# Who multiplies Q and K with the rope's cosines in layer 1: VectorE or GpSimd

## The chip, the cores and the metric

The kernel runs on one core of a Trainium2 chip. The metric is the device time of one execution in microseconds; less is better. The core's engines run side by side, each with an instruction stream of its own, and wait for one another on semaphores: TensorE (PE in the profile) for matrix products, VectorE (DVE), ScalarE (ACT), GpSimd (POOL), and SyncE (SP), which issues DMAs.

## The reference, cut to what matters

Two transformer layers over 1024 tokens of width 256. Each layer is attention (16 heads of 16) and then a mixture of 32 experts with 4 per token, each behind a layer norm, with a residual added. Only layer 1's attention turns Q and K by the rope:

```python
def _apply_rope(x, sin, cos):
    xp = x.reshape(x.shape[:-1] + (x.shape[-1] // 2, 2))
    swapped = jnp.stack((-xp[..., 1], xp[..., 0]), axis=-1).reshape(x.shape)
    return x * cos + swapped * sin
...
q = jnp.einsum('bsd,hkd->bhsk', x, wq.reshape(H, dk, D))   # k, v likewise
sin, cos = _rope_tables(S, dk, THETA, x.dtype)
q = _apply_rope(q, sin, cos)
k = _apply_rope(k, sin, cos)
scores = jnp.einsum('bhqk,bhsk->bhqs', q, k) / jnp.sqrt(jnp.asarray(dk, x.dtype))
```

So for each of Q and K there are a swap of neighbours, a product with sines, a product with cosines, and a sum. After it come causal scores, softmax, the product with V, and the output projection.

## The kernel before, in words

The loop `for L in range(2)` in each engine's stream runs the two layers. Q and K are kept transposed: 256 rows (head dimensions) by 1024 tokens, in two blocks of 128 rows, `m` = 0 and 1. `qkf(m, j)` is block `m` of Q (`j` = 0) or of K (`j` = 1), 128x1024 in f32. Block 0 lies in memory that the profile calls w_sgu, block 1 in xn. Head groups 0 and 1 live in block 0, groups 2 and 3 in block 1.

In layer 1 the work around the change goes so, and each engine does its share strictly in this order:

- TensorE makes block 0's Q and K in four products of 512 tokens (L830), then V for 8 token tiles (L846), then block 1's Q and K in four more (L830), and after that the maxima of the scores (L875, L878) for head group 0.
- ScalarE copies the four products of block 0 out of PSUM (L1234). Each copy adds 1 to the semaphore `qk_sb1`. It then goes through a fixed list: the first bf16 part of Q (`split`, L1246), V's tiles 0 to 3 (`v_out`, L1253), the second part of Q, V's tiles 4 to 7, the first part of K, and one copy of block 1, the second part of K, and the other copies of block 1.
- VectorE turns block 0 (L1519 to L1528): first Q, then K. For each it waits for two copies, shuffles neighbours into `swapped` (L1516), multiplies with the sines (L1526), multiplies with the cosines into `by_cos` (L1527), and adds (L1528), which adds 1 to `roped`. Between K's shuffle and K's sines it takes the first part off Q (`take_part`, L302). After K's sum it takes the remaining parts off Q and K (three more at L302), then shuffles Q of block 1, and then reads score maxima out of PSUM (L1556).
- GpSimd waits for the last of these `take_part`s (`left`), and then turns block 1 by itself: cosines (L710), sines (L712), sum (L714), for Q and for K. Between layer 0's last expert and that wait it has nothing to do.
- SyncE sends the bf16 parts of block 0 to QA and KA by DMA (L539), each as soon as ScalarE or VectorE has made it, in the order Q first part, Q second, K first, Q third, K second, K third. Head group 0's maxima wait for all of these.

`ch.step` gives an instruction a semaphore increment; `ch.link` does the same and makes the engine wait for it before its next instruction. The VectorE stretch, with the helper that takes a part off:

```python
def take_part(eng, L, m, j, part):                                   # L296
    eng.wait_ge(S(f"parts_p{part}_{L}"), 2 * m + j + 1)
    q = qkf(m, j)
    eng.tensor_tensor(q if part == 1 else by_rows(part_of(m, j, 2)), q, by_rows(part_of(m, j, part - 1)),
                      ALU.subtract)\
       .then_inc(left(L, m, j, part)[0], 1)                          # L302
...
dve.wait_ge(S("rope"), 32)                                           # L1519
for j in range(2):
    q, by_sin = qkf(0, j), by_rows(swapped[:, j, :])
    dve.wait_ge(S("qk_sb1"), (j + 1) * NC)                           # NC = 2
    ch.link(turn_pairs(j, 0))                                        # the shuffle
    if j == 1:
        take_part(dve, 1, 0, 0, 1)
    ch.step(v.tensor_tensor(by_sin, by_sin, by_rows(sin_t[:, :]), ALU.mult))
    ch.link(v.tensor_tensor(by_rows(by_cos[:, j, :]), q, by_rows(cos_t[:, :]), ALU.mult))
    v.tensor_tensor(q, by_rows(by_cos[:, j, :]), by_sin, ALU.add).then_inc(S("roped"), 1)
take_part(dve, L, 0, 0, 2)
take_part(dve, L, 0, 1, 1)
take_part(dve, L, 0, 1, 2)
```

Other lines that the rows name: L732 is GpSimd's causal mask over a block of probabilities. L769 to L784 (GpSimd) and L1792, L1873 (VectorE) make layer 0's token lists. L1625 and L1630 (VectorE) belong to layer 1's RMS norm. L1294 is ScalarE's exponential.

Of the kernel before, what the change touches and what calls it, by code (L numbers as in the profile page):

```python
# [10 lines left out]
ALU = mybir.AluOpType  # L11
# [13 lines left out]
NC = T // CH  # L25
# [252 lines left out]
def build(nc, a, out):  # L278
    ctx = ExitStack()
    with ctx:  # L280
        sems = {}

        def S(name):
            if name not in sems:
                sems[name] = ctx.enter_context(nc.semaphore(name))
            return sems[name]

        def left(L, m, j, part):

            who, those = ("pool", POOL_PARTS) if (m, j) in POOL_PARTS else ("dve", DVE_PARTS)  # L290
            return S(f"left{part}_{who}"), len(those) * L + those.index((m, j)) + 1
# [6 lines left out]
# [8 lines that stand above are left out]
        def sb(name, shape, dt=F32):  # L306
            return ctx.enter_context(nc.sbuf_tensor(name, shape, dt))
# [29 lines left out]
        cos_t = sb("cos_t", [P, T])  # L337
        sin_t = sb("sin_t", [P, T])
# [14 lines left out]
        def by_rows(t):  # L353

            return t.rearrange("p (c n) -> p c n", n=D)
# [6 lines left out]
        def qkf(m, j):  # L362

            return xn[:, TPC * j:TPC * (j + 1), 0:D] if m else qk_first[:, j, :, :]
# [9 lines left out]
        by_cos = X[:, 2 * T:4 * T].rearrange("p (a t) -> p a t", a=2)  # L374
# [278 lines left out]
        def _(pool):  # L653
            ch = Chain(pool, S("pool_own"))
# [43 lines left out]
            for L in range(2):  # L698
# [3 lines left out]
                if L == 0:  # L702
                    ch.link(pool.memset(V[:, :, :, DH + 1:], 0.0))
                    pool.memset(V[:, :, :, DH:DH + 1], 1.0).then_inc(S("v_pad"), 1)
                else:

                    pool.wait_ge(*left(1, 0, 1, 2))
                    for j in range(2):
                        pool.wait_ge(S("qk_sb1"), (2 + j + 1) * NC)
                        ch.step(pool.tensor_tensor(by_rows(cos_late), qkf(1, j), by_rows(cos_t[:, :]), ALU.mult))  # L710
                        pool.wait_ge(S("swapped"), j + 1)
                        ch.link(pool.tensor_tensor(by_rows(swapped_late[:, j, :]), by_rows(swapped_late[:, j, :]),  # L712
                                                   by_rows(sin_t[:, :]), ALU.mult))
                        pool.tensor_tensor(qkf(1, j), by_rows(cos_late), by_rows(swapped_late[:, j, :]), ALU.add)\  # L714
                            .then_inc(S("roped"), 1)
                        pool.wait_ge(S("roped"), 2 + j + 1)
                for j in range(2):
                    take_part(pool, L, 1, j, 1)
                for st, (_, _, c, b) in enumerate(STEPS):
                    if L == 0 and st == PHASE_AT[4]:  # L720

                        pool.wait_ge(S("qa_rows0_3"), 16 * 2 * NPROD)
                        pool.memset(bias_parts, 0.0).then_inc(S("bias_parts"), 1)
                    if not DIAGONAL[st]:
                        continue
                    if st in (2, 3):

                        take_part(pool, L, 1, st - 2, 2)
                    off = b * P - c * CH
                    block_p = probs[:, st % PB, :, off:off + P]  # L730
                    pool.wait_ge(S(f"exp{L}"), 2 * st + 2)
                    pool.affine_select(out=block_p, in_=block_p, compare_op=ALU.is_ge, fill=0.0, base=0,  # L732
                                       pattern=[[0, HG], [1, P]], channel_multiplier=-1).then_inc(S(f"masked{L}"), 1)
# [66 lines left out]
        def _(pe):  # L800
# [17 lines left out]
            for L in range(2):  # L818
# [44 lines left out]
                def unit(x):  # L863
# [3 lines left out]
                    if n >= RB:  # L867
                        pe.wait_ge(*out_of(UNITS[n - RB]))
                    if x[0] == "max":
                        _, g, u = x  # L870
                        _, i, h0, nh, s0, w = MAX_UNITS[u]
                        for j in range(nh):
                            h = HG * g + h0 + j
# [3 lines left out]
                            if diag:  # L877
                                mm = pe.matmul(ps[:, bank, (j + 1) * w - P:(j + 1) * w], identb[:, :], mask_q[:, :],  # L878
                                               start=False, stop=True)
                    elif x[0] == "rows":  # L880
                        _, g, c = x
                        pe.wait_ge(S(f"neg_max{L}"), PHASES.index((g, c)) + 1)
                        for i in range(TPC):
# [552 lines left out]
        def _(dve):  # L1436
            ch = Chain(dve, S("dve_own"))
            v = nc.vector
# [60 lines left out]
            for L in range(2):  # L1499
# [13 lines left out]
                def turn_pairs(j, m):  # L1513

                    swap = [x ^ HG for x in range(32)]
                    return v.stream_shuffle(by_rows((swapped_late if m else swapped)[:, j, :]), qkf(m, j), swap)  # L1516

                if L == 1:
# [3 lines that stand above are left out]
                        dve.wait_ge(S("qk_sb1"), (j + 1) * NC)  # L1522
                        ch.link(turn_pairs(j, 0))
                        if j == 1:
                            take_part(dve, 1, 0, 0, 1)
                        ch.step(v.tensor_tensor(by_sin, by_sin, by_rows(sin_t[:, :]), ALU.mult))  # L1526
                        ch.link(v.tensor_tensor(by_rows(by_cos[:, j, :]), q, by_rows(cos_t[:, :]), ALU.mult))  # L1527
                        v.tensor_tensor(q, by_rows(by_cos[:, j, :]), by_sin, ALU.add).then_inc(S("roped"), 1)  # L1528
                if L == 0:
                    take_part(dve, 0, 0, 0, 1)  # L1530
# [541 lines left out]
```

## Time and profile before

| | us |
|---|---|
| median of 3 runs | 777.88 |
| lowest and highest of them | 777.22, 784.95 |
| the profiled execution's own time | 778.84 |
| its span, first to last instruction | 777.1 |

The profiled execution is one more run, 0.96 us above the median; 1.7 us of it lie outside the span. All rows below are of this execution, and their times count from its span's start. A row of a timeline gives the start, the time until the end, the engine and line, and in square brackets how long the engine had been idle before it and what ended that. Rows with xN merge N instructions that follow each other; starts and ends are then of the whole.

### The profile page before, as it was taken

The page shows a single profiled execution, that of the slowest core. Times are in us where ns is not written, and L with a number is a line of the kernel's source. Part 1 is how long each engine was busy: PE and PEld are TensorE (multiplying, and loading weights), DVE is VectorE, ACT ScalarE, POOL GpSimd, SP SyncE. Part 2 cuts the span into 40 slices and gives each one's busy share as a digit, 9 for nine tenths or more (in the row PEclk, how much of TensorE's full clock was granted, in tenths as well). Part 3 has the DMA queues.
Part 4 walks back from the last instruction along what each step waited for, and adds up shares of the span by engine and source line. Part 5 has one row for each costly group of instructions (what it writes and reads, how often), then busy time and mean ns, then how long its engine had stood idle before and what let it go on. Part 6 is the DMA issues. An engine that isn't in the chain of part 4 may idle for free.

```text
span 777.1 us, 13393 instructions
## 1 busy us (share of the span) xinstructions
PE 676.1 (87%) x4375; PEld 438.1 (56%) x4375; DVE 487.7 (63%) x1357; ACT 323.1 (42%) x684; POOL 250.5 (32%) x293
## 2 busy tenths in 40 slices
PE   3988999999578999999963978999998899999981
PEld 2533443345347999999842533343343456999970
DVE  4489899454683444444466889899526885343447
ACT  3553465764124333222331533564676231333322
POOL 3140111211047776444410183010211002677620
PEclk9999999999679999999996979999999999999995
DMA  3443210150009999999770244003000530499662
GB/s 98 139 132 110 77 35 0 44 175 28 27 29 301 322 322 312 299 299 306 228 228 0 88 134 159 15 4 113 2 1 1 183 113 15 138 293 305 217 222 70
DMA packets 60263, 108.54 MB, mean 140 GB/s; under 512 B 11173, under 2 KB 37115, under 8 KB 60068
## 3 DMA queue, kind: packets, MB, share of 16 engines
q1 hardware_dynamic: 52500, 93.86, 37.6%
q0 software_dynamic: 7632, 13.80, 5.5%
q8 instruction: 37, 0.61, 0.3%
q14 instruction: 30, 0.25, 0.1%
q10 hardware_dynamic: 64, 0.03, 0.0%
HBM read 79.98 MB, written 19.79 MB: 128 GB/s over the span
## 4 chain that ended last, share of the span: by engine, by line
PE 56%; DVE 25%; DMA 6%; ACT 4%; issue 4%; POOL 2%; SPq 1%; ACTq 0%; POOLq 0%; DVEq 0%
PE ps L1125 13%; DVE mx L1556 11%; PE ps L957 7%; PE ps L943 6%; PE ps L875 5%; PE ps L1138 4%; PE ps L989 4%; PE ps L1140 4%; DMA outs<-X,token 3%; PE ps L1069 3%; ACT X L1294 2%; PE ps L908 1%; PE ps L1101 1%; SPq L539 1%; PE ps L830 1%
## 5 line engine op out<-in xcount | busy, mean ns | idle before, releaser
L1556 DVE TENSOR_REDUCE mx<-ps 128x1 f32<-128x512 f32 (+3 forms) x304 | 180.5, 656 | 25.9 <-PE ps L878 17.5
L1294 ACT ACTIVATE X<-ps 128x1024 f32<-128x1024 f32 (+1 forms) x192 | 146.6, 809 | 87.9 <-PE ps L943 87.5
L875 PE MATMUL ps<-KA,QA 112*128 112x512 bf16 (+3 forms) x384 | 113.1, 345 | 8.6 <-DVE mx L1556 3.9
L760 POOL DMA_INDIRECT outs<-X,token x95 | 95.0, 1000 | 73.6 <-DVE X L1929 59.4
L732 POOL TENSOR_SCALAR_AFFINE_SELECT X<-X 128x512 f32<-128x512 f32 x64 | 40.9, 639 | 219.0 <-ACT X L1294 219.0
L943 PE MATMUL ps<-QA,KA 114*128 114x512 bf16 (+3 forms) x384 | 93.8, 330 | 5.9 <-ACT X L1294 4.0
L1125 PE MATMUL ps<-QA,KA 128*128 x756 | 95.0, 275 | 1.9 <-ACT QA L1400 1.5
L1125 PEld LDWEIGHTS ps<-QA,KA 128*128 128x128 f32 x756 | 91.9, 192 | 4.6 <-issue 2.8
L1916 DVE TENSOR_TENSOR X<-ps,X 128x128 f32<-128x128 f32 x95 | 27.7, 292 | 101.4 <-ACT X L1411 101.0
L752 POOL DMA_INDIRECT V<-token_rows,row_of_slot x64 | 66.8, 1043 | 66.8 <-DVE row_of_slot L1829 42.9
L875 PEld LDWEIGHTS ps<-KA,QA 112*128 112x128 bf16 x384 | 36.9, 100 | 84.9 <-DVE mx L1556 60.6
L957 PE MATMUL ps<-X,V 128*32 128x512 f32 (+3 forms) x768 | 81.1, 497 | 0.4 <-ACT X L1301 0.4
L1409 ACT ACTIVATE X<-ps 128x128 f32<-128x128 f32 x95 | 26.4, 278 | 117.2 <-PE ps L1125 117.2
L943 PEld LDWEIGHTS ps<-QA,KA 114*128 114x128 bf16 x384 | 30.2, 99 | 49.8 <-ACT X L1294 30.8
L1138 PE MATMUL ps<-KA,X 128*128 128x256 f32 x190 | 57.1, 382 | 0.7 <-DVE X L1920 0.2
L1140 PE MATMUL ps<-X 128*128 128x256 f32 x190 | 56.5, 379 | 0.0
L989 PE MATMUL ps<-xT,w_sgu 128*128 128x512 f32 x112 | 54.2, 628 | 2.2 <-DVE QA L1700 2.2
L1929 DVE COPY X<-ps 128x256 f32<-128x256 f32 x95 | 40.4, 425 | 20.5 <-DMA outs<-X,token 16.3
L878 PE MATMUL ps<-mask_q,identb 128*128 128x128 bf16 x256 | 51.9, 230 | 0.0
L1125 PE MATMUL ps<-X,KA 128*128 128x128 f32 x384 | 48.2, 275 | 0.3 <-ACT X L1400 0.3
L1125 PEld LDWEIGHTS ps<-X,KA 128*128 128x128 f32 x384 | 45.6, 192 | 0.6 <-ACT X L1400 0.5
L1140 PEld LDWEIGHTS ps<-X 128*128 128x128 f32 x190 | 36.1, 190 | 4.9
(288 smaller groups left out, 870.8 us busy)
## 6 DMA issues: line engine op xcount, KB each, us to landing
KA<-in_ex SPq DMA_DIRECT2D x95, 512.0 KB
X<-in_dn SPq DMA_DIRECT2D x95, 64.0 KB
outs<-empty SPq DMA_DIRECT2D x4, 1024.0 KB, 9.9
V<-outs SPq DMA_DIRECT2D x4, 1024.0 KB, 5.7
QA<-X SPq DMA_DIRECT2D x28, 128.0 KB, 2.5
KA<-X SPq DMA_DIRECT2D x28, 128.0 KB, 2.5
QA<-w_sdn SPq DMA_DIRECT2D x28, 128.0 KB, 2.5
KA<-parts_k SPq DMA_DIRECT2D x28, 128.0 KB, 2.4
```

Of the source, the lines that this page charges most:

```text
L752: pool.indirect_dma_start(out=rows[:, g % ROW_RING, :], out_offset=None, in_=token_rows[L], in_offset=bass.IndirectOffsetOnAxis(ap=row_of_ ...
L760: pool.indirect_dma_start(out=outs[L], out_offset=bass.IndirectOffsetOnAxis(ap=token[L][:, i:i + 1], axis=0), in_=erows[:, g % OUT_RING, : ...
L875: mm = pe.matmul(ps[:, bank, j * w:(j + 1) * w], QA[0:KQ, h, i * P:(i + 1) * P], KA[0:KQ, h, s0:s0 + w], start=True, stop=not diag)
L878: mm = pe.matmul(ps[:, bank, (j + 1) * w - P:(j + 1) * w], identb[:, :], mask_q[:, :], start=False, stop=True)
L943: mm = pe.matmul(ps[:, 4 + 2 * p + x, off:CH], KA[0:KX, h, b * P:(b + 1) * P], QA[0:KX, h, c * CH + off:(c + 1) * CH], start=True, stop=True)
L957: mm = pe.matmul(ps[32 * x:32 * x + 32, RB, off:CH], V[:, b, HG * g + x, :], probs[:, st % PB, x, off:CH], start=(b == 0), stop=(b == TPC ...
L989: mm = pe.matmul(ps[:, up_bank(L, u, x), :], w_sgu[:, k, col:col + P], xT[:, k, n * CH:(n + 1) * CH], start=(k == 0), stop=(k == KD - 1))
L1125: mm = pe.matmul(ps[:, 2 + g % RING, m * P:(m + 1) * P], w_ex[:, r, col:col + P], rowsT_all[:, k, bass.ds(at, P)] if L == 0 else rowsT(L, ...
L1138: pe.matmul(ps[:, 6 + g % 2, 0:D], eact[:, g % RING, 0:P], w_ex[:, r, KD * UPC * P:EW], start=True, stop=False)
L1140: mm = pe.matmul(ps[:, 6 + g % 2, 0:D], eact[:, g % RING, P:2 * P], w_rest[:, r // 2, :], start=False, stop=True)
L1294: nc.scalar.activation(probs[:, st % PB, 2 * p:2 * p + 2, off:CH], ps[:, 4 + 2 * p:6 + 2 * p, off:CH], ACT.Exp, scale=SCALE).then_inc(S(f" ...
L1556: v.tensor_reduce(mx[:, part, i, h0:h0 + nh], ps[:, n % RB, 0:nh * w].rearrange("p (h w) -> p h w", h=nh), AX.X, ALU.max)\
```

## The change: what it does

GpSimd's stream for layer 1 gets two instructions ahead of its wait for `left`: the cosine products of block 0, Q's after two copies and K's after four. They write the same `by_cos`. VectorE's stream loses these two; its sine product is now a `link`, and it waits for GpSimd's semaphore `by_cos` ahead of each sum.

```diff
@@ GpSimd, layer 1
+                    pool.wait_ge(S("rope"), 32)
+                    for j in range(2):
+                        pool.wait_ge(S("qk_sb1"), (j + 1) * NC)
+                        pool.tensor_tensor(by_rows(by_cos[:, j, :]), qkf(0, j), by_rows(cos_t[:, :]), ALU.mult)\
+                            .then_inc(S("by_cos"), 1)
                     pool.wait_ge(*left(1, 0, 1, 2))
@@ VectorE, layer 1
-                        ch.step(v.tensor_tensor(by_sin, by_sin, by_rows(sin_t[:, :]), ALU.mult))
-                        ch.link(v.tensor_tensor(by_rows(by_cos[:, j, :]), q, by_rows(cos_t[:, :]), ALU.mult))
+                        ch.link(v.tensor_tensor(by_sin, by_sin, by_rows(sin_t[:, :]), ALU.mult))
+                        dve.wait_ge(S("by_cos"), j + 1)
                         v.tensor_tensor(q, by_rows(by_cos[:, j, :]), by_sin, ALU.add).then_inc(S("roped"), 1)
```

## Rows read from the trace of the kernel before

**Rows 1.** The chain that ended last, 390 to 450 us: start, length, what.
```profile
428.25 0.61 ACT w_sgu L1234
...
428.99 1.31 DVE X L1516
...
431.55 1.15 DVE X L1527
...
438.74 1.24 DVE w_sgu L1528
440.00 1.07 ACT X L1246
...
445.51 2.63 DMA KA<-X
```

**Rows 2.** The timeline of VectorE, 424 to 450 us.
```profile
432.72 1.23 DVE L1528 TENSOR_TENSOR w_sgu<-X 128x1024 f32<-128x1024 f32 x1
...
433.87 1.30 DVE L1516 STREAM_SHUFFLE X<-w_sgu 128x1024 f32<-128x1024 f32 x1
435.21 1.22 DVE L302 TENSOR_TENSOR w_sgu<-w_sgu,X 128x1024 f32<-128x1024 f32 x1
436.35 1.22 DVE L1526 TENSOR_TENSOR X<-X,sin_t 128x1024 f32<-128x1024 f32 x1
```

**Rows 3.** The timeline of ScalarE, 424 to 450 us.
```profile
431.69 0.60 ACT L1234 ACTIVATE w_sgu<-ps 128x512 f32<-128x512 f32 x1 [1.12 <-PE ps L830]
433.98 1.06 ACT L1246 ACTIVATE X<-w_sgu 128x1024 bf16<-128x1024 f32 x1 [1.70 <-DVE w_sgu L1528]
434.94 1.19 ACT L1253 ACTIVATE V<-ps 128x256 f32<-128x256 f32 x4
...
438.59 0.66 ACT L1253 ACTIVATE V<-ps 128x256 f32<-128x256 f32 x2 [0.52 <-PE ps L846]
```

**Rows 4.** The timeline of GpSimd, 444 to 450 us.
```profile
444.80 2.35 POOL L710 TENSOR_TENSOR X<-xn,cos_t 128x1024 f32<-128x1024 f32 x1 [51.88 <-DVE X L302]
```

**Rows 5.** The timeline of GpSimd, 214 to 232 us.
```profile
217.63 0.18 POOL L770 TENSOR_TENSOR X<-X 32x1 f32<-32x1 f32 x1
217.91 1.08 POOL L771 TENSOR_SCALAR X<-X 32x1 f32<-32x1 f32 x1
...
221.02 1.26 POOL L777 TENSOR_TENSOR X<-X 32x1 f32<-32x1 f32 x1
```

**Rows 6.** The timeline of VectorE, 214 to 232 us.
```profile
217.66 1.23 DVE L1792 TENSOR_TENSOR X<-X,dest 128x1024 f32<-128x1024 f32 x1
...
221.01 1.22 DVE L1873 TENSOR_TENSOR X<-iota_t,X 128x1024 bf16<-128x1024 f32 x1
```

**Rows 7.** The timeline of all engines, 587.5 to 589.2 us.
```profile
586.77 1.57 ACT L1294 ACTIVATE X<-ps 128x768 f32<-128x768 f32 x2
...
588.41 0.64 POOL L732 TENSOR_SCALAR_AFFINE_SELECT X<-X 128x512 f32<-128x512 f32 x1 [3.11 <-ACT X L1294]
...
588.52 0.54 DVE L1625 TENSOR_TENSOR msq<-msq,mv 128x4 f32<-128x4 f32 x1
```

**Rows 8.** The timeline of all engines, 591 to 593 us.
```profile
592.16 0.76 POOL L732 TENSOR_SCALAR_AFFINE_SELECT X<-X 128x512 f32<-128x512 f32 x1 [3.11 <-ACT X L1294]
...
592.34 0.85 DVE L1630 SCALAR_TENSOR_TENSOR xn<-hb,msq,w_nm 128x256 f32<-128x256 f32 x1
```

**Rows 9.** Single lines: durations in ns (min/median/max), first and last start.
```profile
L1625 DVE TENSOR_TENSOR msq<-msq,mv x2: 166/355/544, 588.5 to 619.3; 128x4 f32<-128x4 f32 x2
...
L1630 DVE SCALAR_TENSOR_TENSOR xn<-hb,msq,w_nm x8: 473/480/851, 592.3 to 622.7; 128x256 f32<-128x256 f32 x8
...
L1516 DVE STREAM_SHUFFLE hb<-xn x2: 1286/1292/1298, 444.6 to 455.7; 128x1024 f32<-128x1024 f32 x2
```

**Rows 10.** Busy time by stretch: PE, PEld, DVE, ACT, POOL; then PE's granted clock, DMA share, GB/s.
```profile
448.10:456.00 7.90, 5.77 (x34) 2.93 (x35) 6.84 (x15) 0.00 (x0) 6.06 (x3) 0.74 0.61 185
...
464.00:472.00 8.00, 7.20 (x46) 2.39 (x44) 7.58 (x15) 5.33 (x8) 7.94 (x7) 1.00 0.47 145
```

## The prediction, made before the changed kernel ran

> **What bounds the kernel now.** I read the chain that ended last first, because an engine's share of busy time says nothing about one stage. Between 428.3 and 448.1 us this chain runs through nothing but the stage that is changed: ScalarE's copy of the second product, then VectorE without a pause from 428.99 to 439.97, then ScalarE's bf16 part of K, SyncE's issues, and the landing of the last part in KA [rows 1]. Both cosine products are in it, at 1.15 us each: one at 431.55, its twin for K six microseconds later. So what the change takes from VectorE lies on the path. The engines' own timelines then say who is free. VectorE is busy all through [rows 2]. GpSimd had been idle for 51.88 us when it began its first product at 444.80 [rows 4]. ScalarE works through its list and waits for VectorE only before a bf16 part [rows 3].
>
> **What is removed.** Two VectorE products of 128x1024. Each begins before its predecessor has ended, so each costs the path 1.15 us, not its recorded 1.22: 2.30 us in all [rows 1]. The sum now follows the sine product, with one more semaphore to look at; a linked pair has a gap of some 0.04 us (the cosine product ends at 431.55 + 1.15 = 432.70, the sum starts at 432.72 [rows 1, 2]), and I allow 0.06.
>
> **What is added on GpSimd.** The nearest row is its product of the same size and types, 2.35 us [rows 4]. A start follows ScalarE's end by 0.07: an exponential ended at 586.77 + 1.57 = 588.34, GpSimd's mask started at 588.41 [rows 7]. ScalarE's second copy ends at 428.85 (428.25 + 0.60), the fourth at 431.69 + 0.60 = 432.29 [rows 1, 3]. So Q's cosines run from 428.92 to 431.27, and K's cannot begin before 432.36. GpSimd has nothing else to do then, and nothing is queued behind these two that starts before 444.80. If the two engines ran freely side by side, VectorE would never wait: its sine product would end at 431.55, after GpSimd.
>
> **Do they run freely?** The trace has small cases of the same pairing, and they say no, in both directions. GpSimd's one-element operations take 0.18 us, but two of their kind took 1.08 and 1.26; these began inside VectorE operations with two tensors in SBUF, and ended at 218.99 and 222.28, where VectorE ended at 218.89 and 222.23 [rows 5, 6]. The other way round: a 128x4 VectorE product with two such inputs takes 0.17 elsewhere, but took 0.54 when it was issued 0.11 after a GpSimd mask, and both ended together, at 589.06 and 589.05 [rows 7, 9]. An operation of 0.48 took 0.85 and ended 0.27 after the mask [rows 8, 9]. So whichever starts second stands still until the first is almost through: the blocked one ends its own length, less about 0.2, after the other's recorded end (0.27 against 0.48, 0.01 against 0.17). A shuffle has one tensor input and is spared: the one that ran into GpSimd's product at 444.80 and the later one both took 1.29 to 1.30 [rows 4, 9].
>
> The Trainium skill, "SBUF — State Buffer", section "Who interferes with whom", says the same of a VectorE instruction with two SBUF inputs beside a GpSimd instruction that reads SBUF, and more strictly: whoever issues first holds the pair of ports for the whole instruction. The rows have the blocked one end some 0.2 earlier than that would allow. By the letter of the Trainium skill each of the two blocks below costs 0.2 more, and the sum would be +1.2 instead of +0.8.
>
> **The sum, step by step.** Sines, sums and subtractions all have two SBUF inputs; only shuffles are spared. Q's shuffle runs from 428.99 to 430.30 as before. The sine product is issued then, finds GpSimd's product running, and ends at 431.27 + 1.22 - 0.2 = 432.29 instead of 431.55. The sum is issued 0.06 later, at 432.35, and K's cosines on GpSimd at 432.36. This is a tie, and it decides the sign.
>
> If GpSimd is first, K's cosines run to 432.36 + 2.35 = 434.71, and Q's sum ends at 434.71 + 1.23 - 0.2 = 435.74, where it was 433.95 [rows 2]: 1.8 late. From there GpSimd is out of the way. The shuffle takes 1.33 to the next start and the subtraction 1.14 (433.87 to 435.21 to 436.35 [rows 2]), so the sines start at 438.21, end at 439.43, and the sum ends at 439.49 + 1.24 = 440.73. Before, it ended at 439.98 [rows 1]. That is **0.8 us later**: 1.8 lost on Q, 1.1 won back on K's missing product.
>
> What follows is a shift of the same size. ScalarE's list is just done in time: Q's first part from 435.77 to 436.83, four V tiles 1.19, then Q's second part when the subtraction has ended (438.3), to 439.4, then V's last four in 0.64 and 0.66, to 440.7 [rows 3]. SyncE, GpSimd's block 1 and the score maxima all wait for these same results, and nothing later has a due time of its own.
>
> I take the tie for GpSimd: of the two, the sum has the additional wait in front of it, for which I have only a gap with one wait as measure, and the mask that took 0.76 instead of 0.64 [rows 7, 8], so had itself been held up, still got in ahead of the VectorE operation issued 0.18 after it. The profiled execution becomes 778.84 + 0.8 = 779.6; against the median, which it exceeds by 0.96, that is 777.88 + 0.8 = **778.7 us**.
>
> **Rivals.** *VectorE wins the tie.* Q's sum runs from 432.35 to 433.58. K's cosines, which waited, end at 433.58 + 2.35 - 0.1 = 435.83 (GpSimd resumes some 0.1 early by [rows 5, 6]). K's shuffle runs beside it; the subtraction is issued at 434.9, is blocked, and ends at 435.83 + 1.22 - 0.2 = 436.85, against 436.43. The sines follow to 438.0, the sum to 439.3: 0.65 us faster, 777.2. For it: the margin is 0.01 us of my own arithmetic. Against: the additional wait.
>
> *No blocking between long products,* the change working as written. VectorE's sum would end 2.2 earlier, at 437.8. But ScalarE must empty all of V before it makes K's part, and V's last two tiles come from TensorE, whose products don't move: that pair starts at 438.59 because of TensorE and ends at 439.25 [rows 3]. K's part then starts at 439.25 instead of 440.00. The gain is capped at 0.75 us, 777.1. Against it stand the four blocked operations; for it only that all four were short or met a short one.
>
> *Slower by the clock.* After its pause TensorE gets on average 0.74 of its clock from 448.1 to 456, and 1.00 from 464 on [rows 10], its two levels being 1.2 and 2.4 GHz. The pause that ends at 448.1 would become 0.8 longer. If the lower level lasted through half of the stretch 464 to 472, 3.6 us of its work [rows 10] would take 7.2 in a window of 4: 3.2 us more, with the 0.8 some 782. It decides once the lower level outlasts VectorE's pace there, which is busy 7.58 of 8.0. Against it: the rise comes after 16 us of work, and a shift of 0.8 in the start is a twentieth of that.
>
> **How the numbers follow.** GpSimd first (778.7) 0.5; VectorE first (777.2) 0.33; no blocking (777.1) 0.12; the clock (782) 0.05. The first three span 777.1 to 779.1, the upper end being a blocked operation that needs its whole length after the other's end, twice 0.2 more. The medians and the profiled run of the kernel before already lie 777.22 to 778.84, so I add some 0.9 below and 1.7 above: 776.2 to 780.8, with the clock case left out. About 1% (7.8 us) is what a measurement of this kernel can tell from no change. No case reaches it, so same 0.97, with 0.01 for faster and 0.02 for slower.
>
> **What the profile after would show.** GpSimd: two new products, starting near 428.9 and 432.4. VectorE: Q's sine product recorded as some 2.0 us long instead of 1.22 (blocked); with GpSimd first, Q's sum as some 3.4 long; with VectorE first, that sum normal and the subtraction at L302 some 1.9 long; without blocking, all normal and ScalarE's first part of K starting just behind V's last copy. ScalarE's first part of K starts near 440.8, 439.3 or 439.25 in the three cases. I would be wrong if GpSimd's products were much longer than 2.35, or if the maxima of head group 0 started by another amount late or early than K's part did.

## The result: 0.7 us lost where it was forecast, and more of it 150 us later

The changed kernel takes 782.13 us (median of 20 runs, 778.87 to 786.49). The kernel before, in 20 runs beside it, takes 778.73 (776.39 to 784.95). The ratio is 1.0041, 95% interval 1.0027 to 1.0055: some 3.2 us slower, where the forecast was 0.8, and outside the range that was given. The profiled execution of the changed kernel has a span of 781.6 us.

The chain that ended last in the changed kernel, in the stage of [rows 1] (its lines stand five lower in the file: L1239 is L1234 of before, L1521 is the shuffle L1516, L1531 the sines, L1533 the sum, L1251 the bf16 part):

```profile
429.72 0.60 ACT w_sgu L1239
...
430.45 1.32 DVE X L1521
...
431.80 2.15 DVE X L1531
...
433.97 3.22 DVE w_sgu L1533
...
440.91 1.24 DVE w_sgu L1533
...
442.17 1.06 ACT X L1251
...
447.68 2.49 DMA KA<-X
```

Q's sine product and sum in the same chain of the kernel before:

```profile
430.32 1.23 DVE X L1526
...
432.72 1.17 DVE w_sgu L1528
```

The cosine products are gone from the chain, but the sine product has grown from 1.23 to 2.15 and Q's sum from 1.17 to 3.22. I measure the stage from the end of ScalarE's second copy to the start of its first bf16 part of K: 11.15 us before (428.85 to 440.00), now 430.32 to 442.17, which is 11.85. GpSimd's timeline shows who held VectorE up, and VectorE's own shows by how much:

```profile
430.49 2.36 POOL L710 TENSOR_TENSOR X<-w_sgu,cos_t 128x1024 f32<-128x1024 f32 x1 [36.99 <-ACT w_sgu L1239]
433.82 2.35 POOL L710 TENSOR_TENSOR X<-w_sgu,cos_t 128x1024 f32<-128x1024 f32 x1 [0.97 <-ACT w_sgu L1239]
```

```profile
431.80 2.13 DVE L1531 TENSOR_TENSOR X<-X,sin_t 128x1024 f32<-128x1024 f32 x1
433.97 3.29 DVE L1533 TENSOR_TENSOR w_sgu<-X 128x1024 f32<-128x1024 f32 x1
...
438.52 1.23 DVE L302 TENSOR_TENSOR w_sgu<-w_sgu,X 128x1024 f32<-128x1024 f32 x1
```

GpSimd's products end at 432.85 and 436.17; VectorE's blocked operations end 1.08 and 1.09 after them, at 433.93 and 437.26. GpSimd's second product was issued 0.15 ahead of VectorE's sum. Once GpSimd has finished, the subtraction takes 1.23, where it took 1.22.

So the stage lost 0.70. The two spans differ by 4.5 us (777.1 and 781.6), and the rest of that lies elsewhere. The changed execution was already 1.5 us late when the stage began (second copy's end 428.85 before, 430.32 now), ahead of anything that was changed; and it wins 0.9 back after the first expert product. In between lie 3.2 us. From the first score maximum (449.10 before, 451.29 now) both kernels run in step until 594 us. Then the changed one falls back by 1.6 us, and 20 us later by 1.6 again. Busy time by stretch in the changed kernel (PE, PEld, DVE, ACT, POOL; then PE's granted clock, DMA share, GB/s):

```profile
593.20:596.70 3.50, 1.71 (x12) 0.41 (x13) 3.48 (x9) 2.09 (x3) 0.76 (x1) 1.00 0.00 0
596.70:600.20 3.50, 3.50 (x18) 1.82 (x18) 1.84 (x4) 1.02 (x1) 0.00 (x0) 0.54 0.00 0
600.20:604.80 4.60, 4.60 (x53) 2.86 (x46) 0.30 (x1) 0.90 (x3) 0.64 (x1) 0.98 0.01 2
...
619.00:623.00 4.00, 2.94 (x5) 1.29 (x6) 3.62 (x22) 0.54 (x2) 0.00 (x0) 0.73 0.99 336
623.00:628.00 5.00, 5.00 (x12) 2.18 (x11) 4.16 (x19) 2.13 (x5) 0.00 (x0) 0.87 1.05 319
```

The same stretches behind the pauses in the kernel before:

```profile
594.50:598.00 3.50, 3.48 (x29) 2.28 (x29) 1.85 (x4) 1.41 (x2) 0.00 (x0) 1.00 0.00 0
...
615.50:619.00 3.50, 2.74 (x7) 1.30 (x8) 3.16 (x19) 0.33 (x1) 0.00 (x0) 1.00 0.98 347
619.00:624.00 5.00, 5.00 (x18) 2.39 (x17) 4.36 (x19) 2.79 (x7) 0.00 (x0) 1.00 1.06 331
```

TensorE pauses for 1.75 us at 594.96, until VectorE has normed the experts' first tokens, and for 2.17 at 617.89, until it has made a product of the shared expert. Behind each pause the clock is at its lower level, 1.2 instead of 2.4 GHz, for 3.4 us in all, in two neighbouring rows each (twice 0.46 of 3.5 us and twice 0.02 of 4.6 make 3.4 behind the first). I call this a fall. The kernel before has the same two pauses, 1.75 at 592.77 and 2.17 at 614.09, and its clock stays at 1.00 behind both.

### The profile page after: what moved, and what is told of

Same layout as the page of the kernel before. It is cut to its first block, busy times and chain, and to the rows that moved or that the text cites. A ratio compares the mean times of both kernels' runs of the same rounds, so it can differ in the third digit from the quotient of the medians.

```text
span 781.6 us, 13396 instructions
## 1 busy us (share of the span) xinstructions
PE 679.4 (87%) x4375; PEld 440.0 (56%) x4375; DVE 488.3 (62%) x1355; ACT 322.8 (41%) x684; POOL 253.1 (32%) x295
## 4 chain that ended last, share of the span: by engine, by line
PE 62%; DVE 25%; DMA 4%; ACT 4%; issue 3%; SPq 1%; ACTq 0%; POOL 0%; DVEq 0%; POOLq 0%
PE ps L1130 16%; DVE mx L1561 11%; PE ps L962 7%; PE ps L948 6%; PE ps L880 5%; PE ps L1143 5%; PE ps L1145 5%; PE ps L994 4%; PE ps L1074 3%; ACT X L1299 2%; PE ps L1106 2%; PE ps L835 1%; PE ps L913 1%; SPq L539 1%; DMA outs<-X,token 1%
```

## The experiments

Each ratio is against the kernel before, run on the same chip in the same session, with its 95% interval. The expectations name theories of the excess, that is, of what the measured 3.4 us (782.13 against 778.73) have over the stage's 0.7. D: it is chance in where TensorE's lower clock falls. E: something in the change costs 3 us each time, E1 the delay itself, E2 GpSimd's products or the altered streams.

**null and again: each kernel once more.**

> The kernel before, unchanged, timed against itself. Stage measure, here and below: from the end of ScalarE's second copy of block 0 to the start of its first bf16 part of K; 11.15 us in the profile before, 11.85 after. Theory D (the change costs only what its stage loses, some 0.7 us, and the rest of the measured 3.4 us is chance in where TensorE's lower clock falls): ratio 1.000 with a scatter of some 0.002. Theory E (something in the change costs 3 us each time): ratio 1.000 with a scatter well under 0.002. Both: stage 11.15.

> The changed kernel once more, unchanged. Stage 11.85 by both. Theory D: ratio near 1.001 (0.7 us of 778), inside 0.999 to 1.003. Theory E: ratio 1.004 again (3 us).

null: stage 11.14, ratio 0.9999 (0.9982 to 1.0016). again: stage 11.86, ratio 1.0018 (0.9998 to 1.0038), falls of the clock behind both pauses as in the first profile. Each stage is within 0.01 us of its first profile. The time of again lies nearer to theory D's 1.001 than to theory E's 1.004, which is just outside the interval, and the scatter of null, 1.6 us or 0.002, is that of theory D.

**delay: the stage made longer without GpSimd.**

```diff
 ch.link(v.tensor_tensor(by_rows(by_cos[:, j, :]), q, by_rows(cos_t[:, :]), ALU.mult))
+if j == 1:
+    ch.link(v.tensor_tensor(by_rows(by_cos[:, j, :])[:, 0:2, :], q[:, 0:2, :],
+                            by_rows(cos_t[:, :])[:, 0:2, :], ALU.mult))
```

> The kernel before with one more VectorE operation in the chain: half of K's cosine product is made twice (same values), some 0.65 us on the path, nothing on GpSimd. Stage 11.8 by all. Theory D: ratio 1.001. Theory E1 (a delay of 0.7 us ahead of layer 1's scores is what costs 3 us, through TensorE's pause and clock): 1.004, as the change. Theory E2 (the excess comes from GpSimd's two products or from the altered instruction streams): 1.001 here, 1.004 for the change.

Stage 11.86, as in the changed kernel; ratio 1.0033 (1.0011 to 1.0054), as in the changed kernel; and the clock falls behind the same two pauses. The first of them, by stretch:

```profile
595.00:599.00 4.00, 4.00 (x22) 1.69 (x20) 1.63 (x3) 1.02 (x1) 0.00 (x0) 0.57 0.00 0
```

So the falls need nothing of GpSimd's. The 1.001 that theories D and E2 gave this run lies just outside the interval, the 1.004 of theory E1 inside it.

**vfirst: the tie decided for VectorE.**

```diff
 pool.wait_ge(S("qk_sb1"), (j + 1) * NC)
+if j == 1:
+    pool.wait_ge(S("roped"), 1)
```

> The change, but GpSimd's product of K also waits for Q's sum (roped 1), so that VectorE's sum cannot be blocked by it. Blocking theory: Q's sine product stays blocked (2.1 us long), Q's sum is normal (1.23), the subtraction at L302 is blocked instead (some 1.9 to 2.0 long); stage 11.15 - 0.65 = 10.5. Rival (each sum is late because it waits for GpSimd's semaphore, not because of blocking): the subtraction is 1.22 and K's sum ends later. Time: 0.65 us under before by theory D, ratio 0.999.

The sum is normal and the subtraction is blocked: its end, 438.87, is 1.08 after GpSimd's, 437.79. VectorE's and GpSimd's timelines in this kernel:

```profile
434.05 1.23 DVE L1535 TENSOR_TENSOR w_sgu<-X 128x1024 f32<-128x1024 f32 x1
...
436.55 2.32 DVE L302 TENSOR_TENSOR w_sgu<-w_sgu,X 128x1024 f32<-128x1024 f32 x1
```

```profile
435.42 2.37 POOL L712 TENSOR_TENSOR X<-w_sgu,cos_t 128x1024 f32<-128x1024 f32 x1 [2.48 <-DVE w_sgu L1535]
```

Stage 10.91, shorter than before by 0.24, not by 0.65. GpSimd starts 0.14 after the sum's end (435.28), where I had it waiting at the door already, so its product and the subtraction end later. Ratio 0.9999 (0.9982 to 1.0015).

**q_only and k_only: half of the change each.** In the first GpSimd's loop runs over `j` = 0 alone, in the second over `j` = 1 alone; VectorE keeps the other product, as in the kernel before.

> Half of the change: GpSimd makes Q's cosine product, VectorE keeps K's. Blocking theory: Q's sine product is blocked (2.1 us long, as in the change), but no GpSimd product runs when Q's sum is issued, so the sum is normal (1.23); VectorE reaches the end of Q's sum 0.35 earlier than before, and K's work is as before: stage 11.15 - 0.35 = 10.8. Rival (the loss is the hand-over by semaphore, alike for Q and K): stage half of the change's loss, 11.5. Time: ratio 0.9995 by theory D.

> The other half: GpSimd makes K's cosine product, VectorE keeps Q's. Blocking theory: GpSimd's product begins while VectorE makes Q's cosines, gets in ahead of Q's sum, and Q's sum is some 3.3 us long; Q's sum ends 2.0 later than before, 1.1 comes back on K: stage 11.15 + 0.85 = 12.0, more than the whole change (11.85). Rival (hand-over, alike for both): 11.5. Time: ratio 1.001 by theory D.

The two halves have opposite signs: stage 10.94 with Q's product on GpSimd, 12.05 with K's. In q_only VectorE's sine product is blocked and the sum is not. GpSimd, then VectorE:

```profile
429.53 2.37 POOL L710 TENSOR_TENSOR X<-w_sgu,cos_t 128x1024 f32<-128x1024 f32 x1 [35.88 <-ACT w_sgu L1239]
```

```profile
430.84 2.14 DVE L1532 TENSOR_TENSOR X<-X,sin_t 128x1024 f32<-128x1024 f32 x1
433.02 1.23 DVE L1537 TENSOR_TENSOR w_sgu<-X 128x1024 f32<-128x1024 f32 x1
```

In k_only GpSimd gets in 0.25 ahead of the sum:

```profile
432.79 2.43 POOL L710 TENSOR_TENSOR X<-w_sgu,cos_t 128x1024 f32<-128x1024 f32 x1 [40.18 <-ACT w_sgu L1239]
```

```profile
433.04 3.25 DVE L1537 TENSOR_TENSOR w_sgu<-X 128x1024 f32<-128x1024 f32 x1
```

A loss by hand-over would have been alike in both, so it is the blocking. The ratios, 1.0008 (0.9989 to 1.0027) and 1.0026 (1.0004 to 1.0049), don't follow the stage closely; k_only's profile has no fall behind the pauses and q_only's has both.

**halves: GpSimd only beside operations with one tensor input.** The edit, against the changed kernel's GpSimd stream:

```diff
-for j in range(2):
-    pool.wait_ge(S("qk_sb1"), (j + 1) * NC)
-    pool.tensor_tensor(by_rows(by_cos[:, j, :]), qkf(0, j), by_rows(cos_t[:, :]), ALU.mult)...
+for j, n in ((0, 0), (0, 1), (1, 0)):
+    pool.wait_ge(S("qk_sb1"), j * NC + n + 1)
+    if j == 1:
+        pool.wait_ge(S("roped"), 1)
+    pool.tensor_tensor(by_rows(by_cos[:, j, :])[:, 2 * n:2 * n + 2, :], qkf(0, j)[:, 2 * n:2 * n + 2, :],
+                       by_rows(cos_t[:, :])[:, 2 * n:2 * n + 2, :], ALU.mult).then_inc(S("by_cos"), 1)
...                                  # VectorE makes columns 2:4 of K's product, and waits for by_cos 2 + j
```

> GpSimd works only where VectorE has an operation with one tensor input or none: Q's cosines in two halves of 512 tokens, each behind one ScalarE copy (the second beside Q's shuffle), and the first half of K's beside K's shuffle; VectorE makes the other half of K's. Blocking theory: no VectorE operation is lengthened, K's sum ends 1.15 + 0.5 = 1.65 us earlier than before, but ScalarE's part of K waits for its copies of V, whose last pair needs TensorE: stage shorter by 0.75 only, 10.4. Rival (GpSimd slows any VectorE operation beside it): the shuffles are longer than 1.31, and the stage is 10.8 or more. Time: ratio 0.999.

Both shuffles run beside a GpSimd product. They take 1.32 and 1.33 us, where they took 1.30 before: just over the rival's sign of 1.31, but longer by 0.02 to 0.03 us and not by the 0.9 to 2.1 of the blocked operations. No other VectorE operation is lengthened. GpSimd, then VectorE:

```profile
429.19 1.28 POOL L712 TENSOR_TENSOR X<-w_sgu,cos_t 128x512 f32<-128x512 f32 x1 [0.35 <-ACT w_sgu L1241]
433.23 1.28 POOL L712 TENSOR_TENSOR X<-w_sgu,cos_t 128x512 f32<-128x512 f32 x1 [2.76 <-DVE w_sgu L1540]
```

```profile
429.25 1.32 DVE L1523 STREAM_SHUFFLE X<-w_sgu 128x1024 f32<-128x1024 f32 x1
430.61 1.22 DVE L1534 TENSOR_TENSOR X<-X,sin_t 128x1024 f32<-128x1024 f32 x1
431.87 1.23 DVE L1540 TENSOR_TENSOR w_sgu<-X 128x1024 f32<-128x1024 f32 x1
433.02 1.33 DVE L1523 STREAM_SHUFFLE X<-w_sgu 128x1024 f32<-128x1024 f32 x1
```

VectorE has K's sum ready at 438.59, but ScalarE is still at V, which it got late from TensorE:

```profile
438.86 0.66 ACT L1260 ACTIVATE V<-ps 128x256 f32<-128x256 f32 x2 [1.07 <-PE ps L853]
439.40 1.06 ACT L1253 ACTIVATE X<-w_sgu 128x1024 bf16<-128x1024 f32 x1
```

Stage 10.29, shorter by 0.86: the cap at 0.75, and 0.1 more because ScalarE's part of K starts 0.12 before the recorded end of V's last copy (438.86 + 0.66 = 439.52). Ratio 0.9997 (0.9978 to 1.0017).

**halves_act: the same, with the cap removed.** The edit, in ScalarE's list, against halves:

```diff
 split(0, 0, 1)
 v_out(2)
-v_out(3)
 split(0, 1, 0)
-qk_out(4)
+v_out(3)
 split(0, 1, 1)
+qk_out(4)
```

> As the run with halves, and ScalarE makes the first part of K ahead of the last pair of V's tiles, and the second part of K ahead of the first copy of block 1. If ScalarE's order is the cap: stage shorter by about 1.6, 9.5. If not: as with halves, 10.4. The scores' first maximum starts 1.6 earlier unless SyncE's issues take over. Time: ratio 0.998.

Stage 9.50, as expected; the part of K now waits for VectorE alone:

```profile
439.45 1.06 ACT L1253 ACTIVATE X<-w_sgu 128x1024 bf16<-128x1024 f32 x1 [0.83 <-DVE w_sgu L1540]
```

The first maximum starts 18.64 us after the second copy's end, before 20.25: the 1.6 arrive there. And yet the ratio is 0.9997 (0.9980 to 1.0015), no gain at all, with both falls in its profile.

**fill_before, fill_after, fill_delay, fill_halves: the two pauses filled.** Four kernels (before, the change, delay, halves_act) with idle matmuls on TensorE ahead of the two waits:

```diff
+if x == ("fT", 0, 0) and L == 1:
+    for _ in range(26):
+        pe.matmul(ps[:, bank, 0:P], identb[:, :], identb[:, :], start=True, stop=True)
 if L == 1:
     pe.wait_ge(S("xn_f1"), TPC * (c + 1))
...
 shared_up(1)
+for _ in range(32):
+    pe.matmul(ps[:, RB, 0:P], identb[:, :], identb[:, :], start=True, stop=True)
 shared_up(2)
```

> The kernel before, with idle matmuls (identity times identity, 128x128, results never read) in two pauses of TensorE in layer 1: 26 ahead of its wait for the first normed tokens of the experts (a pause of 1.75 us), 32 ahead of the third shared product (2.17 us). In the profile after, TensorE's granted clock was at its lower level for 3.4 us right behind each of these pauses, which cost 1.6 and 1.7 us; in the profile before it was not, though the pauses are as long. Theory D (the excess over the stage's 0.7 us is these falls, which come in some executions and not in others): no fall behind the two pauses, scatter smaller, time as before or up to 1.5 us less. Theory E2 (the excess lies elsewhere): as before.

> The change, with the same idle matmuls in the two pauses. Theory D: against the run fill_before the difference is the stage's loss alone, 0.7 us, and no fall behind the pauses. Theory E2 (the excess comes from elsewhere in the change): 2 to 3 us over fill_before.

> The run delay (half of K's cosine product made twice on VectorE, nothing on GpSimd), with the same idle matmuls. Theory D: 0.7 us over fill_before, where the run delay was 2.4 us over before. Theory E1 (the delay costs TensorE clock in other places): 2 us over fill_before.

> The run halves_act (GpSimd beside shuffles only, ScalarE's order changed; its stage was 1.65 us shorter, its time that of before), with the same idle matmuls. Theory D: 1.65 us under fill_before, ratio against before 0.996 to 0.998: the fastest of all. Theory E (any change of the timing loses 1 to 2 us elsewhere): no faster than fill_before.

The medians are of 12 runs each, of 7 for fill_halves.

| | median, us | ratio, 95% interval | stage, us |
|---|---|---|---|
| fill_before | 776.84 | 0.9964 (0.9945 to 0.9984) | 11.13 |
| fill_after | 777.22 | 0.9964 (0.9942 to 0.9985) | 11.86 |
| fill_delay | 778.02 | 0.9982 (0.9969 to 0.9996) | 11.88 |
| fill_halves | 774.45 | 0.9937 (0.9916 to 0.9959) | 9.50 |

In none of the four profiles does the clock fall behind these pauses. fill_after, TensorE's timeline and then by stretch:

```profile
592.77 1.62 PE L920 MATMUL ps<-identb 128*128 128x128 bf16 x26
594.59 0.66 PE L929 MATMUL ps<-identf,xn 128*128 128x128 f32 x4 [0.20 <-DVE xn L1640]
```

```profile
592.50:596.00 3.50, 3.30 (x38) 2.62 (x36) 3.31 (x8) 1.31 (x2) 0.57 (x1) 1.00 0.00 0
...
616.00:620.00 4.00, 3.67 (x9) 1.76 (x10) 3.56 (x23) 1.28 (x3) 0.00 (x0) 1.00 0.99 343
```

Now the change costs 0.4 us by the medians (777.22 - 776.84), 0.3 by the means, and the scatter of 12 runs each leaves 1.1 to either side. In the profiles, from the second copy's end to the end of the span, it costs 0.70: 345.65 (775.4 - 429.70, before rounding) against 344.95, which is the stage's loss. fill_delay is 1.2 over fill_before by the medians and 1.5 by the means, between the 0.7 and the 2 of the two theories. fill_halves is 2.4 under it by the medians, 1.3 by the means, and the intervals of the two overlap; at 0.63% under the kernel before it has the lowest median of all the kernels tried, and is faster than the kernel before.

One result fits neither theory. Theory D gave fill_before up to 1.5 us; it is 2.9 us faster by the means than the kernel before (779.85 in 30 runs beside it), although no profile of the kernel before has a fall behind the two pauses. The profiles of the two don't show the gain at the pauses either: from the end of the first pause to the first expert product both take 69.6 us. Of the 3.4 us between their spans (777.1 and 773.7), 1.6 lie ahead of the first pause's end and 1.8 behind the first expert product. In the first of these the clock differs too: the kernel before has a fall behind a pause of 2.06 us that ends at 475.14, and in the profile of fill_before the 8 us from 472 have 1.00. The kernel before:

```profile
472.00:480.00 8.00, 5.77 (x38) 2.98 (x36) 6.55 (x14) 0.59 (x1) 0.76 (x2) 0.79 0.53 168
```

So the kernel before has falls that come and go as well, at a place that neither the change nor a filler touches. What the fillers gain in it stays open.

**again2, again3, null2, null3: does the change bring the falls, or chance?**

> The changed kernel once more, beside the kernel before on the same chip, with again3, null2 and null3: two profiles and two sets of times of each. If the falls of TensorE's clock behind the pauses at some 592.8 and 614.1 us come by chance, in both kernels alike: the mean of again2 and again3 lies 0.7 us (0.0009) over that of null2 and null3, within 0.0015, and the falls stand in some of the four profiles without regard to the kernel. If the change itself brings them: 2 to 3 us (0.0025 to 0.004) over, falls in both profiles of the change, and in neither of the kernel before.

> The kernel before, unchanged, as the other side of again2 and again3; expectations stand there. Ratio 1.000.

> The changed kernel, second set beside again2; expectations stand there.

> The kernel before, second set beside null2; expectations stand at again2.

Ratios: again2 1.0042 (1.0024 to 1.0060), again3 1.0027 (0.9998 to 1.0056), null2 1.0012 (0.9996 to 1.0029), null3 1.0008 (0.9993 to 1.0024). The change's 23 runs have a mean of 781.81, the 24 of the kernel before 780.05: 1.8 apart, give or take 1.4, between the two expectations and compatible with both. The profiles: both falls in again2, none in again3, none in null2 and null3. The kernel before (null3), then again2, in the stretches with the first pause and behind it:

```profile
589.30:592.80 3.50, 1.75 (x14) 0.66 (x15) 3.47 (x9) 1.65 (x3) 0.75 (x1) 1.00 0.00 0
592.80:596.30 3.50, 3.50 (x31) 2.29 (x29) 1.42 (x3) 1.41 (x2) 0.00 (x0) 1.00 0.00 0
```

```profile
590.50:594.00 3.50, 2.00 (x14) 0.39 (x13) 3.39 (x11) 2.61 (x4) 0.75 (x1) 1.00 0.00 0
594.00:597.50 3.50, 2.98 (x14) 2.09 (x18) 1.81 (x5) 1.01 (x1) 0.00 (x0) 0.57 0.00 0
```

Over all profiles without filler: the falls stand in none of four of the kernel before, in three of four of the change, and in five of six of the other variants, among them four whose stage is shorter than before; k_only is the sixth. From the first score maximum to the first expert product there are 215.0 us in each of the four of the kernel before, 217.9 to 218.2 in the change's three with falls, and 214.8 in the one without.

## Why the prediction was wrong, point by point

**Right: what bounds the stage, and the blocking.** The row pairs [rows 5 to 9] carried over from 0.6 us operations to 2.35 us ones. The sine product was forecast at 2.0 us and measured at 2.13, Q's sum at 3.4 and 3.29, the subtraction untouched. q_only, k_only and vfirst show that blocking is the cause: in each the operations that had been named beforehand were blocked, and no others.

**Right: the tie went to GpSimd, but it was no tie.** I had 0.01 us between the two issues; it was 0.15. After its long wait GpSimd began Q's cosines 0.17 behind ScalarE's copy, not 0.07, so the sine product ended later, while K's cosines did start 0.07 behind the fourth copy (433.75 to 433.82). The reason that I gave, the additional wait ahead of the sum, did not decide it: the sum was issued 0.04 behind the sine product's end, as between linked operations before. The side was right by luck.

**Right: the sum of the stage,** 0.8 forecast, 0.70 measured, and within 0.02 of that in three further profiles. The sum let the shuffle start only at the recorded end of Q's sum; it starts 0.08 earlier, before (433.87 against 433.95) and after, which is about the difference. A blocked operation resumes some 0.15 before the other's recorded end (1.08 after it, against its own 1.22 or 1.23), where I took 0.2. By the letter of the rule in the Trainium skill ("SBUF — State Buffer", section "Who interferes with whom") it would be nothing; these rows are nearer to that than mine were, and don't reach it. By that letter the sum would have been +1.0 and not the +1.2 that I gave, and the upper end 778.9 and not 779.1: K's cosines would still have started at 432.36, so a later end of the sine product only shortens the wait of Q's sum, and the 0.2 counts once.

**Right: ScalarE's cap.** The rival without blocking was capped at 0.75 by V's last tiles. halves has its K part directly behind V's last copy, and halves_act shows that the order of that list was the cap.

**Wrong: "What follows is a shift of the same size" and "nothing later has a due time of its own".** This step put everything behind the stage at a shift of 0.8, and left out the clock behind pauses that stay as they are. Two pauses of TensorE, which end 145 and some 168 us behind the first score maximum, cost 1.6 us each in an execution where its clock falls behind them, and nothing where it doesn't. Shown: in the change's three profiles with falls, the way from the first maximum to the first expert product is 2.9 to 3.2 us longer, and delay, with no product on GpSimd there, has the same 3.2. With the pauses filled there are no falls in four profiles, and fill_after's times lie 0.3 us over those of fill_before, give or take 1.1. That the excess of the 20 runs is these falls rests on this; the changed kernel without fillers was not timed beside them. I did price a loss of this kind, 3.2 us by the clock, but in the wrong place, 464 to 472 us, where the profile after again has 1.00, and with a chance of 0.05; that the size came out alike is chance. The evidence was in reach: I took the clock to be at 1.00 from 464 on, where the kernel before's own trace has the 0.79 of 472 to 480 that is shown above.

**Open: why the falls came with the change, and how often.** Its timeline from the first maximum to the first pause is that of the kernel before, so what differs is only when the pause comes. The Trainium skill, "TensorE: Matmul & The Clock Gate", Part 1, says that the clock's activity window is free-running and doesn't restart with a kernel; no run here shows that by itself. If that alone decided, the falls would come by chance, alike in both kernels. The counts of the profiles speak against that: none of four against eight of ten for kernels whose stage had been shifted either way. But k_only and again3 escaped the falls too. Nor can it be a time, counted from the start, that the kernel before keeps and the others miss: its first maximum starts anywhere from 447.00 to 451.97 us in the four profiles, and that of the change from 449.45 to 451.29. The mean granted clock, on record for each execution, says that the profiles overstate the contrast. Two falls take 0.0044 off it (an estimate: 3.4 us at half the clock, twice, in 780). If all of the change's executions had them and none of the kernel before's, its mean would be lower by that; it is lower by 0.0005 in the session of again (12 executions against 47) and by 0.0016 in that of again2 and again3 (23 against 58), each give or take some 0.002. So the falls are more frequent with the change, if they are, by less than the profiles suggest, and why is not shown.

## What to carry to other kernels

Before work is handed from VectorE to GpSimd beside it, count the SBUF tensor inputs of what VectorE runs meanwhile: K's product, which ran almost wholly beside two-input operations, cost 0.90 us for the 1.15 that it spared VectorE; Q's, which ran half beside a shuffle, gained 0.21; beside shuffles or an idle VectorE the cost was 0.03 at most. Where a change of under 1 us comes back as 3, compare the granted clock of both traces behind TensorE's pauses, also far from the change, and measure the stage itself: its 0.70 came back in every profile, while the times, with the pauses filled or not, scatter by more than that.

## What I had not expected of the hardware

58 idle matmuls in two pauses made the kernel before 0.36% faster (0.16% to 0.55%), more than any version of the rope did by itself; its profiles do not show where. And pauses of the same length, 1.75 and 2.17 us, at the same place in the work, were followed by the lower clock in some executions and not in others.
